# Gated linear attention outputs made channel-major, with their squares formed on GpSimd and summed over channels by TensorE two tiles later

## The reference, cut to what matters

```python
# chunks of 64 tokens; one head, key size 32, value size 512; S is the state
A = where(tril, einsum('bid,bjd,bijd->bij', q, k, exp(D)), 0)
o = A @ v + (q * exp(B)) @ S
S = S * exp(Blast)[..., None] + einsum('bjd,bjv->bdv', k * exp(Blast - B), v)
# o: 1024 tokens x 512 channels for each batch
go = o @ Wog.T + x @ Wig.T
on = o * rsqrt(mean(o * o, axis=-1) + 1e-5) * g_norm_w
return (on * (go * sigmoid(go))) @ Wo.T
```

## Time and profile before

| | |
|---|---|
| median of 3 runs | 915.43 us (915.24 to 915.91) |
| the profiled execution's own time | 915.74 us |
| its span, first to last instruction | 914.0 us |
| TensorE busy | 893.0 us (98%) |
| weight loads | 719.6 us (79%) |
| VectorE busy | 613.1 us (67%) |
| ScalarE busy | 419.3 us (46%) |
| GpSimd busy | 307.6 us (34%) |
| granted TensorE clock, mean | 0.996 of full speed |

### The profile page before, as it was taken

How to read it: one execution, slowest core, us unless ns; L and a number is a source line. 1 busy time by engine, 2 the same in 40 slices (tenths; PEclk the granted TensorE clock), 3 DMA queues, 4 the chain that set the end, 5 groups by cost and what they waited for, 6 DMA issues and landing times.

```text
span 914.0 us, 13820 instructions
## 1 busy us (share of the span) xinstructions
PE 893.0 (98%) x4978; PEld 719.6 (79%) x4978; DVE 613.1 (67%) x1167; ACT 419.3 (46%) x709; POOL 307.6 (34%) x288
## 2 busy tenths in 40 slices
PE   8999999999999999999999999999999999999994
PEld 7777877876888888888778777888878878888883
DVE  6755754487987798798679647665678786544413
ACT  6544333544444643634574656454643463332222
POOL 3000400004776444434334332231236222733342
PEclk9999999999999999999999999999999999999998
DMA  8632021203110000000010300010201643232411
GB/s 291 180 110 93 13 84 45 81 13 104 41 30 1 0 1 1 1 1 1 2 45 1 105 1 1 3 46 1 93 2 26 190 156 101 69 116 73 145 61 46
DMA packets 43974, 54.21 MB, mean 59 GB/s; under 512 B 6113, under 2 KB 25858, under 8 KB 43906
## 3 DMA queue, kind: packets, MB, share of 16 engines
q1 hardware_dynamic: 42082, 49.11, 16.9%
q0 software_dynamic: 1824, 4.22, 1.4%
HBM read 42.78 MB, written 10.52 MB: 58 GB/s over the span
## 4 chain that ended last, share of the span: by engine, by line
PE 67%; DVE 3%; issue 3%; ACT 2%; POOL 1%; DVEq 0%; ACTq 0%; POOLq 0%
PE ps L41 15%; PE ps L43 14%; PE ps L42 14%; PE ps L2390 8%; PE ps L2391 8%; DVE acc L1782 2%; PE ps L2525 2%; PE ps L2436 1%; PE ps L2532 1%; PE ps L2542 1%; PE ps L2508 1%; POOL p_lo L2223 1%; PE ps L2499 1%; PE ps L2668 0%; PE ps L2614 0%
## 5 line engine op out<-in xcount | busy, mean ns | idle before, releaser
L1782 DVE SCALAR_TENSOR_TENSOR acc<-ps,gu_scale,acc 128x512 f32<-128x512 f32 x264 | 197.5, 749 | 48.2 <-ACT acc L1447 28.4
L2390 PE MATMUL ps<-xt_hi,gu_val 128*128 128x512 f32 x352 | 140.6, 399 | 3.2 <-PEq L71 1.5
L2391 PE MATMUL ps<-xt_lo,gu_val 128*128 128x512 f32 x352 | 137.3, 390 | 0.0
L1447 ACT ACTIVATE acc<-ps,gu_scale 128x512 f32<-128x512 f32 x88 | 60.7, 689 | 89.5 <-PE ps L2391 89.4
L2295 POOL TENSOR_TENSOR fsg<-fsg,acc 128x512 f32<-128x512 f32 x44 | 58.8, 1337 | 108.8 <-DVE acc L1782 104.8
L2390 PEld LDWEIGHTS ps<-xt_hi,gu_val 128*128 128x128 f32 x352 | 66.0, 188 | 28.2 <-DVE acc L1782 11.2
L2391 PEld LDWEIGHTS ps<-xt_lo,gu_val 128*128 128x128 f32 x352 | 66.1, 188 | 12.2
L2300 POOL TENSOR_TENSOR fh_lo<-fsg,fh_hi 128x512 fp32r<-128x512 f32 x44 | 59.0, 1340 | 42.7 <-ACT fh_hi L1459 42.7
L41 PE MATMUL ps<-dn_hi,fh_hi 128*128 128x512 f32 x172 | 67.6, 393 | 0.0
L42 PE MATMUL ps<-dn_hi,fh_lo 128*128 128x512 f32 x172 | 67.1, 390 | 0.0
L43 PE MATMUL ps<-dn_lo,fh_hi 128*128 128x512 f32 x172 | 67.0, 390 | 0.0
(11 more groups left out here) (321 smaller groups left out, 2130.8 us busy)
## 6 DMA issues: line engine op xcount, KB each, us to landing
mw_raw<-in_w SPq DMA_DIRECT2D x16, 512.0 KB, 3.6
a_nib<-in_gate_up_packed SPq DMA_DIRECT2D x88, 64.0 KB, 2.6
x<-x SPq DMA_DIRECT2D x16, 256.0 KB, 2.8
mw_raw<-x SPq DMA_DIRECT2D x8, 512.0 KB, 4.2
out<-mw_raw SPq DMA_DIRECT2D x8, 512.0 KB, 3.0
xt_raw<-in_xT SPq DMA_DIRECT2D x3, 1024.0 KB, 4.8
x<-in_x SPq DMA_DIRECT2D x3, 1024.0 KB, 5.5
a_nib<-in_down_packed SPq DMA_DIRECT2D x8, 256.0 KB, 3.4
```

The lines of the kernel that those rows point to most:

```text
L1447: act.activation(acc[part][u // 2 % 2][:, :], ps[:, FG, :], ACT.Copy, scale=gu_scale[:, part * IT + j, 0:1]).then_inc(s_g0, 1)
L1782: dve.scalar_tensor_tensor(out=a[:, :], in0=ps[:, FG + c, :], scalar=gu_scale[:, part * IT + j, c:c + 1], in1=a[:, :], op0=ALU.mult, op1=A ...
L2390: pe.matmul(ps[:, FG + c, :], gu_val[:, o, c, :], xt_hi[b % 2][:, c, :], start=True, stop=False)
L2391: pe.matmul(ps[:, FG + c, :], gu_val[:, o, c, :], xt_lo[b % 2][:, c, :], start=False, stop=True).then_inc(s_gu, 1)
```

## The change

Five things are done together.

1. `outputs` swaps its operands: x and `state` are stationary, `at` and `q_rows` moving, so o comes out with channels on the partitions. `take_o`, `square_o`, `transpose_o` and `o_tok` are gone. `o_high` and `o_low` read the output banks themselves; `o_low` is what frees them (`outputs_left`, where `s_ot` stood). `o_low(t-1)` moves ahead of the other VectorE work of tile t.
2. GpSimd gets `sum_squares` behind each `join_o`: the square of the joined tile (512 elements in each partition), the sum of its halves (256) and the sum of what is left (128), each waiting for the one before. TensorE then sums over the partitions with one product with a column of ones (`total_squares`), in tile t for tile t-2, the last two around `gate_o(n, 0)`. `mean_square` reads its result in PSUM and stands behind `gated(n, 0)`; `inverse_rms` stands behind `p_low(n, 0)`.
3. `pair_t` has 128 partitions in place of 64, the upper half set to zero once by GpSimd, so `scores` contracts over 128 rows.
4. The low part of the fourth gated group (m = 3) of blocks 0 to 2 goes from GpSimd to VectorE (`third_p_low`).
5. The low part of the very last hidden tile goes from GpSimd to VectorE.

Cut to the changed lines (declarations of semaphores left out):

```diff
@@ -1072,11 +1072,11 @@
-        pair_t = [put(f"pair_t{i}", [2 * DK, 2, P], 84 + i) for i in range(2)]
+        pair_t = [put(f"pair_t{i}", [P, 2, P], 150 + i) for i in range(2)]
...
-        o_tok = put("o_tok", [P, C], 184)
+        sq = [put(f"o_squares{i}", [P, KC, P], at_) for i, at_ in enumerate((184, 102))]
@@ -1085,7 +1085,6 @@
-        junk_a = sg[0]
@@ -1096,7 +1095,6 @@
-        ss = [sb(f"gss{i}", [P, TB]) for i in range(2)]
@@ -1312,6 +1312,14 @@
+        def out_chunks(n):
+            if n == 0:
+                return ps[:, 3:5, 0:2 * P].rearrange("p a (h c) -> p h a c", c=P)
+            return ps[:, 0:4, 0:P]
...
+        def chunks_of_tile(n, tile):
+            return tile.rearrange("p (h a) c -> p h a c", a=2) if n == 0 else tile
@@ -1494,7 +1502,7 @@
-                act.activation(pair_t[t % 2][:, :, :].rearrange("d a n -> d (a n)"), ps[0:2 * DK, feature_bank(n, t), 0:2 * P], ACT.Copy).then_inc(s_pt, 1)
+                act.activation(pair_t[t % 2][0:2 * DK, :, :].rearrange("d a n -> d (a n)"), ps[0:2 * DK, feature_bank(n, t), 0:2 * P], ACT.Copy).then_inc(s_pt, 1)
@@ -1503,43 +1511,19 @@
-            def take_o(n, t):
+            def o_high(n, t):
...
-                act.wait_ge(s_ott, i)
-                act.wait_ge(s_ss, i)
-                act.wait_ge(s_pl, KC * n)
-                if n == 0:
-                    chunks_out, chunks_in = "p (h a c) -> p a h c", ps[:, 3:5, 0:2 * P].rearrange("p a (h c) -> p a h c", c=P)
-                    act.activation(o_tok[:, :].rearrange(chunks_out, a=2, c=P), chunks_in, ACT.Copy).then_inc(s_ot, 1)
-                else:
-                    act.activation(o_tok[:, :].rearrange("p (j c) -> p j c", c=P), ps[:, 0:4, 0:P], ACT.Copy).then_inc(s_ot, 1)
...
-            def square_o(n, t):
-                i = TB * n + t
-                act.wait_ge(s_ot, i + 1)
-                act.wait_ge(s_pl, KC * n)
-                if i == 0:
-                    act.wait_ge(rows.s_ss, TB * NBLK)
-                if n >= 2:
-                    act.wait_ge(s_rms, n - 1)
-                act.activation(junk_a[:, :], o_tok[:, :], ACT.Square, accum_out=ss[n % 2][:, t:t + 1]).then_inc(s_ss, 1)
...
-            def o_high(n, t):
-                i = TB * n + t
-                act.wait_ge(s_ott, i + 1)
...
-                act.activation(o_hi[:, :, t * P:(t + 1) * P], ps[:, OT, :].rearrange("p (m n) -> p m n", m=KC), ACT.Copy).then_inc(s_oh, 1)
+                act.activation(chunks_of_tile(n, o_hi[:, :, t * P:(t + 1) * P]), out_chunks(n), ACT.Copy).then_inc(s_oh, 1)
...
             def silu(n, m):
...
-                    act.wait_ge(s_ss, TB * n + TB)
-                elif m == 3:
-                    act.wait_ge(s_ott, TB * n + TB)
+                elif m >= 2:
@@ -1651,25 +1635,16 @@
-                    if t:
-                        square_o(n, t - 1)
...
-                    if t:
-                        o_high(n, t - 1)
...
-                    take_o(n, t)
+                    o_high(n, t)
...
-                    o_high(0, TB - 1)
...
-                    o_high(n, TB - 1)
-                else:
-                    o_high(n, TB - 1)
-                square_o(n, TB - 1)
@@ -1878,19 +1853,24 @@
             def o_low(n, t):
...
-                dve.tensor_tensor(o_lo[:, :, t * P:(t + 1) * P], ps[:, OT, :].rearrange("p (m n) -> p m n", m=KC),
-                                  o_hi[:, :, t * P:(t + 1) * P].bitcast(F32), ALU.subtract).then_inc(s_ol, 1)
+                dve.tensor_tensor(chunks_of_tile(n, o_lo[:, :, t * P:(t + 1) * P]), out_chunks(n),
+                                  chunks_of_tile(n, o_hi[:, :, t * P:(t + 1) * P].bitcast(F32)), ALU.subtract).then_inc(s_ol, 1)
...
             def mean_square(n):
...
-                dve.tensor_scalar(ms[:, :], ss[n % 2][:, :], 1.0 / C, GLA_EPS, ALU.mult, ALU.add).then_inc(s_ms, 1)
+                dve.tensor_scalar(ms[:, :], ps[:, OT, 0:TB], 1.0 / C, GLA_EPS, ALU.mult, ALU.add).then_inc(s_ms, 1)
...
+            def third_p_low(n):
+                dve.wait_ge(s_ph, KC * n + 4)
+                dve.wait_ge(s_pl, KC * n + 3)
+                dve.tensor_tensor(p_lo[:, 3, :], sg[3][:, :], p_hi[:, 3, :].bitcast(F32), ALU.subtract).then_inc(s_pl, 1)
@@ -2094,6 +2074,8 @@
+                    if t:
+                        o_low(n, t - 1)
@@ -2105,8 +2087,6 @@
-                    if t:
-                        o_low(n, t - 1)
@@ -2115,13 +2095,10 @@
-                else:
-                    q_shift(1)
-                    k_plus_one(1)
...
-                    k_inverse(1)
-                mean_square(n)
+                    q_shift(1)
+                    k_sigmoid(1)
@@ -2136,6 +2113,7 @@
+                mean_square(n)
@@ -2158,6 +2136,8 @@
+                if n < LAST:
+                    third_p_low(n)
@@ -2194,6 +2174,10 @@
+            dve.wait_ge(m_hh, FT * NB)
+            dve.wait_ge(m_hl, FT * NB - 1)
+            dve.wait_ge(m_y, (FT - 1) * (NB - 1) + FT - HS)
+            dve.tensor_tensor(h_lo[(FT - 1) % HS][:, :], h[(FT - 1) % 2][:, :], h_hi[(FT - 1) % HS][:, :].bitcast(F32), ALU.subtract).then_inc(m_hl, 1)
@@ -2207,6 +2191,19 @@
+            def sum_squares(n, t):
...
+                i = TB * n + t
+                q = sq[t % 2]
+                pool.wait_ge(s_of, i + 1)
+                if i >= 2:
+                    pool.wait_ge(s_ss, i - 1)
+                pool.tensor_tensor(q[:, :, :], o_f[:, :, t * P:(t + 1) * P], o_f[:, :, t * P:(t + 1) * P], ALU.mult).then_inc(s_osq, 1)
+                pool.wait_ge(s_osq, i + 1)
+                pool.tensor_tensor(q[:, 0:2, :], q[:, 0:2, :], q[:, 2:4, :], ALU.add).then_inc(s_osh, 1)
+                pool.wait_ge(s_osh, i + 1)
+                pool.tensor_tensor(q[:, 0, :], q[:, 0, :], q[:, 1, :], ALU.add).then_inc(s_osc, 1)
@@ -2313,6 +2310,11 @@
+            pool.wait_ge(s_ftt, 1)
+            for u in range(2):
+                pool.memset(pair_t[u][2 * DK:P, :, :], 0.0).then_inc(s_pz, 1)
+            pool.wait_ge(s_pz, 2)
@@ -2323,6 +2325,7 @@
+                    sum_squares(n, t)
@@ -2334,27 +2337,27 @@
-                inverse_rms(n)
...
+                inverse_rms(n)
...
-                    p_low(n, 3)
...
-                for j in range(FT):
+                for j in range(FT if b < NB - 1 else FT - 1):
...
+            between(NB - 1, FT - 1)
@@ -2448,9 +2451,12 @@
+            def outputs_left(i):
+                pe.wait_ge(s_ol, i)
...
             def transpose_qk(n):
...
-                pe.wait_ge(s_ot, TB * n)
+                outputs_left(TB * n)
@@ -2505,13 +2511,15 @@
+                if i < 2:
+                    pe.wait_ge(s_pz, i + 1)
...
             def outputs(n, t):
...
-                pe.wait_ge(s_ot, i)
+                outputs_left(i)
@@ -2522,25 +2530,23 @@
-                        ins = pe.matmul(ps[:, bank, cols], at[t % 2][:, :], x[n][:, t, j * P:(j + 1) * P], start=True, stop=first)
+                        ins = pe.matmul(ps[:, bank, cols], x[n][:, t, j * P:(j + 1) * P], at[t % 2][:, :], start=True, stop=first)
...
-                            ins = pe.matmul(ps[:, bank, cols], q_rows[t % 2][d, :], state[1 - t % 2][d, :], start=False, stop=True)
+                            ins = pe.matmul(ps[:, bank, cols], state[1 - t % 2][d, :], q_rows[t % 2][d, :], start=False, stop=True)
...
-            def transpose_o(n, t):
+            def total_squares(n, t):
...
-                pe.wait_ge(s_ot, i + 1)
-                pe.wait_ge(s_ol, i)
-                for m in range(KC):
-                    ins = pe.transpose(ps[:, OT, m * P:(m + 1) * P], o_tok[:, m * P:(m + 1) * P], const.ident[:, :])
-                ins.then_inc(s_ott, 1)
+                pe.wait_ge(s_osc, i + 1)
+                pe.wait_ge(s_ms, n)
+                pe.matmul(ps[:, OT, t:t + 1], sq[t % 2][:, 0, :], const.ones[:, 0:1], start=True, stop=True).then_inc(s_ss, 1)
@@ -2557,7 +2563,7 @@
-                    pe.wait_ge(s_ot, TB * n + TB)
+                    outputs_left(TB * n + TB)
@@ -2594,7 +2600,7 @@
-                    pe.wait_ge(s_ot, TB * NBLK)
+                    outputs_left(TB * NBLK)
@@ -2604,9 +2610,9 @@
-                    pe.wait_ge(s_ol, TB * NBLK)
-                    pe.wait_ge(s_ot, TB * NBLK)
+                    outputs_left(TB * NBLK)
...
+                    pe.wait_ge(s_ms, NBLK)
@@ -2660,8 +2666,8 @@
             def broadcast_scores(b, bank):
...
-                    pe.wait_ge(s_ot, TB * LAST)
-                    pe.wait_ge(s_ol, TB * LAST)
+                    outputs_left(TB * LAST)
+                    pe.wait_ge(s_ms, LAST)
@@ -2720,10 +2726,10 @@
-                    if t:
-                        transpose_o(n, t - 1)
...
+                    if t >= 2:
+                        total_squares(n, t - 2)
@@ -2732,14 +2738,15 @@
-                transpose_o(n, TB - 1)
...
+                total_squares(n, TB - 2)
...
+                total_squares(n, TB - 1)
```

## The result

The changed kernel takes 908.99 us (median of 4 runs, 908.78 to 909.50), the kernel before 915.58 beside it; the ratio is 0.9928, with a 95% interval of 0.9915 to 0.9942. The profiled execution took 909.50 us, with a span of 907.6. So 6.6 us came off where 5.65 were forecast; the time lies 0.8 us under the forecast of 909.8.

A forecast was written before the change was run, and what follows sets the result against it. TensorE, busy for 98%, was taken as the bound. Terms -5.9 - 0.7 + 0.2 + 1.1 - 0.35 = -5.65 us from the profiled 915.74 gave 910.1, or 909.8 as median; own range 907.5 to 912.5, 8 in 10 905.8 to 913.3.

The forecast's parts named there:

- Transposes less sums: TensorE, 16 tiles: removed transposes of o take 7.0 us off, added sum-of-squares products put 3.7 us on.
- Scores over 128 rows: TensorE's score products: one 128-row setting saves 0.16 us a tile (0.06 to 0.30), 2.6 us in all.
- 0.22 apart: Sign of being right: in the trace the pair of score products would stand 0.22 us apart.
- The old wait on `o_low` in block 0: TensorE's wait before block 0's first gate product with o would go: 0.7 us off.
- The old wait at the turn to block 1: TensorE's 1.21 us wait for group 3's low part would stay, 0.2 us longer.
- VectorE's key work behind GpSimd: Turn to block 1: VectorE's key work standing behind GpSimd would delay what TensorE waits for by 0.8 us.
- Block 3: Full GpSimd makes tile 1's sum about 0.6 us late and delays `o_low(3, 3)`: together 1.1 us on, 0 to 3.5.
- The end: Program's end: TensorE's wait for the last low part shrinks with VectorE making it, 0.35 us off.
- A: Rival: all new waits hidden, old wait around block 1 gone, scores save 1 us more: 906.3 us; chance 0.18.
- B: Rival: small products and switch cost more, GpSimd holds up each block's key chain: 914.2 us; chance 0.15.
- C: Rival: VectorE operations reading SBUF wait out two or more GpSimd operations, 2.6 us at least: 922.6 us; chance 0.10.
- D: Rival: scores over 128 rows save nothing: 912.4 us; counted within the forecast's 0.57.

The follow-up runs named there:

- run 4: Changed kernel with scores over 64 rows again and both low parts back on GpSimd, leaving the outputs change alone: 912.66 us, ratio 0.9970.
- run 5: Changed kernel with each tile's one-column products for the sum of squares issued twice: 912.78 us, ratio 0.9968.
- Experiment 3: Kernel before with only the two low parts (third group of blocks 0 to 2, last hidden tile) moved from GpSimd to VectorE: 914.84 us, ratio 0.9992.
- Experiment 6: Changed kernel with GpSimd's square of each tile made twice: 915.46 us, ratio 0.9999.
- experiment 9: Changed kernel with Silu earlier in block 0, tile 1's sum and a rank later in block 3, and GpSimd's square made twice: 917.59 us, ratio 1.0023.
- run 1: Changed kernel with its scores read over 64 rows again, nothing else changed: 911.90 us, ratio 0.9961.
- run 2: Kernel before with only the scores read over 128 rows, lower 64 zeroed once by GpSimd: 913.06 us, ratio 0.9972.

## Why the prediction was right, point by point

- **Transposes less sums.** Forecast 0.44 - 0.23 a tile. Runs 4 and 5 give 0.24 for the sum (0.255 in the trace), and 0.20 for both together: 3.2 us in all, as the sum had it.
- **Scores over 128 rows.** Forecast 0.16 a tile and 2.6 us in all; measured 0.14 in block 2 in both kernels, and 2.65 and 2.9 us in all. The size is right, but the two terms behind it came out otherwise, and their errors cancel: I put the pair at 0.22 us to the next operation and the step ahead of it at up to 0.14 us more than before. The step ahead stayed at 0.35, and the pair takes 0.33 us before a transpose and 0.24 before a product of 512 columns, so the sign "0.22 apart" did not come in blocks 1 and 2. The Trainium skill, "TensorEngine Tiling (Array Packing)", section "Key Properties", says that a change of the tiling mode drains TensorE. In the changed kernel the weight load of the scores still stands idle for 0.2 us in 15 cases, behind updates of 32 columns; so a standstill ahead of the scores is there with either number of rows, and what went lies between their two passes and behind them. In the sixteenth case, the very first tile, the products ahead of the scores are full ones of 128 rows and columns: the load stands idle for 0.37 us there with 64 rows and not at all with 128, and this tile gained 0.4 us. There the trace agrees with the page; for the other fifteen it was not measured that the drain is what went.
- **The old wait on `o_low` in block 0** went, as forecast.
- **The old wait at the turn to block 1.** Forecast 0.2 more; it fell from 1.21 to 0.65, with 0.18 on the rows' low part behind it, so 0.4 less. The step that failed is the reckoned chain: I let it come 2.1 us earlier, and TensorE resumed 3.3 us earlier (560.76 against 564.05). Of these, 2.7 had come by the start of group 3's high part (559.34 against 562.02), about the 1.5 and 1.1 that I had put down as gains, and VectorE's shorter low part gave 0.6. So nothing is left for the 0.8 us that I took off for VectorE's key work behind GpSimd; no run measures that term by itself. Experiment 3 shows that the new place of the low part gives 0.4 of the wait; the rows' low part behind it, forecast at 0.3, is there with its 0.18.
- **A wait that no view listed.** The low part on VectorE also gave 0.33 us at the turn to block 3. It wasn't in the sum. A step of 0.45 in a row of 0.23 in the trace of the kernel before would have shown it.
- **Block 3.** Forecast 1.1 us of waits, with the sum of tile 1 0.6 late and `o_low(3, 3)` behind. Measured 0.51 and 0.26 listed; the stretch gained 0.63 where four tiles and the 0.33 would give 1.7, so 1.1 us were lost there. So the 1.1 us were met, and the two places are those named, but in part by luck: 0.3 of the loss stands at no listed wait, and GpSimd's period was 4.96 and not 5.45:

```profile
676.69 1.30 POOL L2193 TENSOR_TENSOR o_f<-o_hi,o_lo 128x512 f32<-128x512 f32 x1
678.07 1.04 POOL L2202 TENSOR_TENSOR o_squares<-o_f 128x512 f32<-128x512 f32 x1
...
681.65 1.30 POOL L2193 TENSOR_TENSOR o_f<-o_hi,o_lo 128x512 f32<-128x512 f32 x1
```

  The square takes 1.04 us where I took the 1.28 of an operation with two different inputs, and the DMA with its gap 1.2 instead of 1.4; the small sums are at 0.73 and 0.46 as reckoned. Experiment 6 shows what one microsecond more a tile would have done: the forecast stood nearer to an edge than its term of 1.1 told.
- **The end.** Forecast 0.35; TensorE got it, the span 0.14 to 0.16. The step that failed is that the span follows TensorE. The tail on VectorE starts 0.45 us earlier, and a new idle time ahead of its last tile takes about two thirds of that back.
- **The sum.** 3.2 + 2.65 + 0.6 + 0.4 + 0.33 + 0.14 - 1.1 = 6.2 of the 6.6 us measured; 0.4 stays without a place. Forecast were 5.65: most of the difference is the wait at the turn to block 1 (0.6) and the unlisted one (0.33), less 0.2 at the end.
- **Rivals.** A needed both waits of block 3 away; they were 0.5 and 0.3. B's price of a sum, 0.31, is refuted by run 5. C's mechanism exists (runs 6 and 9). In the changed kernel no outputs started late for VectorE's sake: beside two GpSimd operations in a row, at 565.76 and 567.13, VectorE's two-input operation got in between, 1.39 us where the earlier trace rows has 0.74. But the sign of being wrong, a VectorE operation over more than one of GpSimd's, did come once there, in block 3's gate, beside an indirect DMA (694.15) and a low part of GpSimd (695.37 to 696.68); TensorE has no wait behind it:

```profile
695.17 2.07 DVE L1868 TENSOR_TENSOR gsg<-gsg,o_f 128x512 f32<-128x512 f32 x1 [0.19 <-ACT gsg L1528]
```

  And C's premise is too wide, as is the rule in my part on GpSimd and VectorE: not every VectorE operation that reads SBUF only waits. The long compares of a rank do not. Beside the join of 676.69 one took 0.74 us, and 0.73 just before it. D is refuted by runs 1 and 2.

## What to carry to other kernels

Where one engine is busy for 98%, read its start-to-start times in a stretch without waits: here the price of each edit came out to 0.03 us a tile, and the three parts, run alone, added up to the whole. Before giving work to a second engine, compare its period for a tile with that of the bound at the tightest place. Here it was shorter (4.96 us against 5.2 and 5.4), and moved orders hid what was left, 1.5 us. With the second square it was longer (6.1), and the same orders only moved the wait to the last sum; that is one pair of runs, not a law. Look for the head of a queue that waits while ready work stands behind it; Silu behind a high part was such a place.

## What the runs showed of the hardware that I had not expected

- A standstill of TensorE can cost more than its length: behind waits of 2.74, 2.82 and once 1.86 us its products ran 0.43 us apart instead of 0.23 for some microseconds (1.5 us lost in experiment 6; in block 0 of experiment 9 nine steps took 551.53 - 547.78 = 3.75 us, 1.6 more than the same steps in experiment 6, at full clock); behind another wait of 1.85 us nothing of it was seen.
- The hold-up between GpSimd and VectorE goes both ways: a VectorE operation of 2.28 us stretched a GpSimd join from 1.28 to 3.24, and small VectorE operations of 0.22 to 0.35 us took 0.93 to 2.07 beside GpSimd. In the rows looked at, VectorE's compares and its operations that read PSUM kept their time (0.74 us for a compare at 676.68 beside a join, and a low part of 0.68 us at 679.51 beside GpSimd's sums).
- GpSimd's product of a tile with itself takes 1.04 us, a sum of two tiles of the same size 1.28.
